# Hats in four groups of 32 rows, spreads in four row groups, one band ahead of the sampling

## What is computed

```python
x = x + _L0_conv_ref(_ln_c(x), ...)     # offsets o1, o2 and mask m by a 3x3 convolution of _ln_c(x)
...
sampled = (v00 * (1 - dy) * (1 - dx) + v01 * (1 - dy) * dx + v10 * dy * (1 - dx) + v11 * dy * dx) * mask
out = jnp.einsum('bkcp,fck->bfp', col, w).reshape(B, F, H, W)
...
t = _to_tokens(x)
t = t + _L0_ffn_ref(_ln_t(t), ...)      # softmax over 8 experts, the best two, gelu, weighted sum
```

## Time and profile before

| what | us |
|---|---|
| median of 3 runs (402.83 to 403.0) | 402.97 |
| span of the profiled execution, first to last instruction | 400.1 |
| what lies around the span, against the median | 2.9 |
| TensorE busy in the span | 315.2 |
| GpSimd busy | 228.9 |
| VectorE busy | 227.3 |
| ScalarE busy | 195.6 |

### The profile page before, as it was taken

The page is one execution under the profiler, slowest core; times in us unless marked ns, Lnnn a source line. Parts: engine busy times, 40 slices in busy tenths (PEclk is TensorE's granted clock), DMA queues, the critical chain, the costliest instruction groups (busy, mean ns, idle before and its releaser), DMA issues.

```text
span 400.1 us, 9901 instructions
## 1 busy us (share of the span) xinstructions
PE 315.2 (79%) x2395; PEld 264.9 (66%) x2395; DVE 227.3 (57%) x988; ACT 195.6 (49%) x526; POOL 228.9 (57%) x351
## 2 busy tenths in 40 slices
PE   0999799999999999999999995049989797885000
PEld 0354688888889888898898994038867686774000
DVE  3983257878778787787887876502222122332085
ACT  1253566565565665756656652314444444442063
POOL 4013043777777777777777766204777777777300
PEclk9999899999999999999999999558999999999555
DMA  8958612222222222222222220855777777762298
GB/s 209 274 164 249 265 54 75 89 80 100 78 93 85 82 99 78 90 94 76 98 84 83 95 80 26 145 139 169 223 222 243 230 231 232 227 221 72 82 315 234
DMA packets 52450, 57.88 MB, mean 145 GB/s; under 512 B 6892, under 2 KB 40423, under 8 KB 52424
## 3 DMA queue, kind: packets, MB, share of 16 engines
q1 hardware_dynamic: 45031, 48.16, 39.1%
q0 software_dynamic: 4544, 8.44, 6.6%
q10 hardware_dynamic: 2848, 0.99, 1.4%
HBM read 30.70 MB, written 14.97 MB: 114 GB/s over the span
## 4 chain that ended last, share of the span: by engine, by line
PE 53%; SPq 16%; issue 10%; DMA 6%; ACT 4%; DVE 4%; POOL 2%; ACTq 2%; DVEq 1%; POOLq 0%
PE bank L1326 18%; PE bank L1315 15%; SPq L481 5%; PE bank L1248 5%; SPq L490 4%; SPq L496 3%; DMA wide<-result 2%; PE bank L1279 2%; PE bank L1433 2%; ACT samp L758 2%; PE bank L1269 2%; PE bank L1260 2%; POOL result L658 2%; DMA routed<-padding_sb 1%; DMA result<-y,to 1%
## 5 line engine op out<-in xcount | busy, mean ns | idle before, releaser
L658 POOL DMA_INDIRECT result<-y,to x78 | 76.8, 985 | 43.8 <-DVE to L1191 26.8
L1326 PE MATMUL bank<-filt_sb,samp 128*128 128x128 f32 x576 | 79.3, 283 | 4.1 <-ACT samp L758 2.5
L1326 PEld LDWEIGHTS bank<-filt_sb,samp 128*128 128x128 f32 x576 | 69.1, 191 | 18.1 <-ACT samp L758 14.2
L1315 PE MATMUL bank<-S,xwin 100*128 100x144 f32 x512 | 78.9, 298 | 1.8 <-issue 1.7
L602 POOL DMA_INDIRECT routed<-payload,slot x64 | 63.2, 987 | 18.5 <-issue 13.5
L758 ACT ACTIVATE samp<-bank 128x432 f32<-128x432 f32 (+1 forms) x96 | 46.3, 484 | 52.8 <-PE bank L1315 52.8
L1315 PEld LDWEIGHTS bank<-S,xwin 100*128 100x128 f32 x512 | 67.7, 193 | 2.2 <-issue 2.0
L923 DVE TENSOR_TENSOR S<-ysp,bank 100x512 f32<-100x512 f32 (+1 forms) x96 | 52.5, 550 | 22.9 <-ACT ysp L729 21.8
L1433 PE MATMUL bank<-rowsT,w_blk 128*128 128x256 f32 x156 | 44.4, 408 | 13.3 <-DMA w_blk<-w_all 10.2
L1199 DVE TENSOR_TENSOR y<-bank,w_blk 128x256 f32<-128x256 f32 x39 | 16.6, 425 | 66.0 <-PE bank L1442 64.2
L822 ACT ACTIVATE rowsT<-bank 128x256 f32<-128x256 f32 x39 | 15.0, 384 | 61.0 <-PE bank L1424 61.0
(11 more groups left out here) (110 smaller groups left out, 493.1 us busy)
## 6 DMA issues: line engine op xcount, KB each, us to landing
w_blk<-w_all SPq DMA_DIRECT2D x39, 321.0 KB
xwin<-lines SPq DMA_DIRECT2D x64, 120.0 KB
xwin<-lines SPq DMA_DIRECT2D x32, 160.0 KB
rows_in<-routed SPq DMA_DIRECT2D x39, 129.0 KB
wide<-result SPq DMA_DIRECT2D x16, 256.0 KB, 4.8
w_all<-in_experts SPq DMA_DIRECT2D x4, 642.0 KB, 7.4
out_tiles<-res SPq DMA_DIRECT2D x8, 256.0 KB, 4.6
wide<-in_x_rows SPq DMA_DIRECT2D x3, 512.0 KB, 8.6
```

The lines of the kernel that those rows point to most:

```text
L658: nc.gpsimd.indirect_dma_start(result, bass.IndirectOffsetOnAxis(to[:, slot, j:j + 1].bitcast(U32), 0), y[:, slot, j, :], None, bounds_che ...
L1315: last = nc.tensor.matmul(bank[5 + (par + g) % 2][:, i * TAPS * TT:(i + 1) * TAPS * TT], xwin[:, par, t, :], weights[:, t], start=True, st ...
L1326: last = nc.tensor.matmul(bank[7][:, 0:C], samp[:, par, j, :], filt_sb[:, order[j], :], start=(j == 0), stop=(j == TAPS - 1))
```

## The change

The three parts of the hats lie in groups of 32 rows: y and x of an even tap, y and x of an odd tap, 30 rows used in each, so that the transposed hats fill 128 rows and not 120. A spread uses only the 30 rows of its group, as stationary and as moving operand. The two wide units are issued as four matmuls behind one another, and the spreads stand one band ahead of the sampling: step b spreads band b + 1. The narrow unit comes after the samples, and then the hat transposes of band b + 2. Hats, high part and split move ahead by one band too, scatter and rows of places come one band later. The place counts lie in bank 4, not in bank 7 beside the projection. VectorE's normalise writes both copies of the payload itself, into a ring of four, and GpSimd only stamps the row numbers. The diff, cut to what the loop and its start do:

```diff
-SLOT = PARTS * HATS
+GROUP = 32
+SLOT = 2 * GROUP
...
-    spread = np.zeros((2, PARTS, 2, WIN, 2, 2, Q), np.float32)
+    spread = np.zeros((2, 2, GROUP, Q), np.float32)
     q = np.arange(Q)
-    for odd in range(2):
-        for part in range(PARTS):
-            spread[odd, part, 0, q % WIN, odd, 0, q] = 1
-            spread[odd, part, 1, q // WIN, odd, 1, q] = 1
-    spread = spread.reshape(2 * SLOT, 4 * Q)
+    for part in range(PARTS):
+        spread[:, 0, part * WIN + q % WIN, q] = 1
+        spread[:, 1, part * WIN + q // WIN, q] = 1
+    spread = spread.reshape(2 * SLOT, Q)
...
-        hat3 = sb("hat3", [P, 2, TAPS + 1, SLOT], BF16)
+        hat3 = sb("hat3", [P, 2, TAPS + 1, 2, GROUP], BF16)
...
-        payload = sb("payload", [P, 2, 2, ROW])
+        payload = sb("payload", [P, QUEUED, 2, ROW])
...
-                nc.gpsimd.tensor_tensor(h3[:, 2], r, h3[:, 1], ALU.subtract).then_inc(s.hat3_ready, 1)
-
-            def pack(b, par):
-
-                pool.wait_ge(s.xn2_ready, b + 1)
-                settle(pool)
-                at_least(pool, (s.scat_even, s.scat_odd)[par], (b // 2) * 32 if isinstance(b, int) else (b - par) * 16)
-                if not isinstance(b, int):
-                    settle(pool)
-                nc.gpsimd.tensor_copy(payload[:, par, :, 0:C], xn2[:, par, :].unsqueeze(1).broadcast_to([P, 2, C])
+                nc.gpsimd.tensor_tensor(lo, r, mid, ALU.subtract).then_inc(s.hat3_ready, 1)
+
+            def stamp(b, q):
+
+                nc.gpsimd.tensor_copy(payload[:, q, :, C:C + 1].bitcast(I32), dest_sb[:, b, :].unsqueeze(2)
                                       ).then_inc(s.payload_ready, 1)
-                nc.gpsimd.tensor_copy(payload[:, par, :, C:C + 1].bitcast(I32), dest_sb[:, b, :].unsqueeze(2)
-                                      ).then_inc(s.payload_ready, 1)
-
-            def scatter(b, par):
+
+            def scatter(b, par, q):
...
+            distances(2, 0)
+            split(2, 0)
+            distances(3, 1)
...
-                distances(2, 0)
-
-                def step(b, par, _):
+                def step(b, par, _, q):
                     known = isinstance(b, int)
-                    if not known or b + 2 < BANDS:
-                        split(b + 2, par)
                     if not known or b + 3 < BANDS:
-                        distances(b + 3, 1 - par)
-                    if not known or b >= 3:
-                        scatter(b - 3, 1 - par)
+                        split(b + 3, 1 - par)
+                    if not known or b + 4 < BANDS:
+                        distances(b + 4, par)
+                    if not known or b >= 4:
+                        scatter(b - 4, par, q)
                     if not known or b >= 2:
-                        pack(b - 2, par)
+                        stamp(b - 2, (q + 2) % QUEUED)
...
+            evacuate_hatT(1)
+            hi_part(2, 0)
...
-                def step(b, par, _):
+                def step(b, par, _, q):
                     known = isinstance(b, int)
-                    if not known or b >= 1:
-                        copy_y(b, par, 0)
-                        copy_y(b, par, 1)
                     if not known or b >= 2:
                         evacuate_tokens(b - 2, par)
-                    if not known or b >= 1:
-                        copy_y(b, par, 2)
+                    if not known or b + 1 < BANDS:
+                        copy_y(b + 1, 1 - par, 0)
+                        copy_y(b + 1, 1 - par, 1)
                     evacuate_samples(b, par, 0)
-                    if not known or b + 1 < BANDS:
-                        evacuate_hatT(b + 1)
                     if not known or b >= 1:
                         std_band(b - 1, 1 - par)
                     evacuate_samples(b, par, 1)
+                    evacuate_samples(b, par, 2)
                     if not known or b + 2 < BANDS:
-                        hi_part(b + 2, par)
-                    evacuate_samples(b, par, 2)
+                        evacuate_hatT(b + 2)
+                    if not known or b + 1 < BANDS:
+                        copy_y(b + 1, 1 - par, 2)
+                    if not known or b + 3 < BANDS:
+                        hi_part(b + 3, 1 - par)
 
...
-                at_least(dve, s.t_psum, b - 1)
-                at_least(dve, s.payload_ready, 2 * (b - 1))
-                nc.vector.tensor_scalar(xn2[:, par, :], x1[:, b, :], mv1[:, par, 0:1], rs1[:, par:par + 1],
+                if not isinstance(b, int) or b >= QUEUED:
+                    dve.wait_ge((s.scat_even, s.scat_odd)[par],
+                                (b // 2 - 1) * 32 if isinstance(b, int) else (b - par) * 16 - 32)
+                nc.vector.tensor_scalar(payload[:, q, :, 0:C], x1[:, b, :].unsqueeze(1).broadcast_to([P, 2, C]),
+                                        mv1[:, par, 0:1], rs1[:, par:par + 1],
                                         ALU.subtract, ALU.mult).then_inc(s.xn2_ready, 1)
...
-                    nc.vector.tensor_tensor(place[:, :], bank[7][:, 256:256 + EXPERTS],
+                    nc.vector.tensor_tensor(place[:, :], bank[4][:, WHERE:WHERE + EXPERTS],
...
+            for link in range(3):
+                hats(2, 0, link)
...
                     other = 1 - par
-                    place_rows(b - 3, other, 0)
-                    if not known or b >= 1:
-                        multiply(b, par, 0)
-                    place_rows(b - 3, other, 1)
-                    if not known or b >= 1:
-                        multiply(b, par, 1)
-                    place_rows(b - 3, other, 2)
+                    place_rows(b - 4, par, 1)
+                    hats(b + 3, other, 0)
+                    place_rows(b - 4, par, 2)
+                    hats(b + 3, other, 1)
+                    place_rows(b - 4, par, 3)
+                    hats(b + 3, other, 2)
                     if not known or b >= 1:
                         multiply(b, par, 2)
-                    place_rows(b - 3, other, 3)
                     residual(b - 1, other, 0)
                     choose(b - 2, par, 0)
-                    hats(b + 2, par, 0)
                     residual(b - 1, other, 1)
                     choose(b - 2, par, 1)
-                    hats(b + 2, par, 1)
+                    residual(b - 1, other, 2)
                     choose(b - 2, par, 2)
-                    hats(b + 2, par, 2)
+                    place_rows(b - 3, other, 0)
+                    if not known or b + 1 < BANDS:
+                        multiply(b + 1, other, 0)
                     choose(b - 2, par, 3)
-                    residual(b - 1, other, 2)
                     choose(b - 2, par, 4)
+                    if not known or b + 1 < BANDS:
+                        multiply(b + 1, other, 1)
                     choose(b - 2, par, 5)
-                    normalise(b - 1, other)
+                    normalise(b - 1, other, (q + 3) % QUEUED)
 
...
             def transpose_hats(b, par):
                 pe.wait_ge(s.hat3_ready, b + 1)
-                if not isinstance(b, int) or b >= 3:
-                    pe.wait_ge(s.route, (b - 3) * 6 + 1)
+                if not isinstance(b, int) or b >= 4:
+                    pe.wait_ge(s.route, (b - 4) * 6 + 1)
+                if not isinstance(b, int) or b >= 5:
+                    pe.wait_ge(s.place_ready, b - 4)
                 for i in range(PAIRS):
                     last = nc.tensor.transpose(bank4b[0:2 * SLOT, i * P:(i + 1) * P],
-                                               hat3[:, par, 2 * i:2 * i + 2, :].rearrange("p k r -> p (k r)"),
+                                               hat3[:, par, 2 * i:2 * i + 2, :, :].rearrange("p k yx r -> p (k yx r)"),
                                                identb_sb[:, :])
                 last.then_inc(s.hatT_psum, 1)
 
-            def spread_hats(b, par, u):
+            def spread_taps(par, u):
+
+                slot, n, odd = (par + u) % 2, UNITS[u], u % 2
+                for yx, arrived in ((0, s.y_psum), (1, s.x_psum)):
+                    first = GROUP * (2 * odd + yx)
+                    rows = slice(first, first + PARTS * WIN)
+                    moving = hatT[rows, 4, :] if u == 2 else hatT[rows, 0:4, :].rearrange("r i t -> r (i t)")
+                    nc.tensor.matmul(bank[2 * yx + slot][0:Q, 0:n], spread_sb[rows, :], moving,
+                                     start=True, stop=True).then_inc(arrived, 1)
+
+            def spread_hats(b, par):
                 pe.wait_ge(s.hatT_ready, b + 1)
-                slot, n, odd = (par + u) % 2, UNITS[u], u % 2
-                moving = hatT[:, 4, :] if u == 2 else hatT[:, 0:4, :].rearrange("r i t -> r (i t)")
-                at_least(pe, s.y_ready, b * 3 + u - 1)
-                nc.tensor.matmul(bank[slot][0:Q, 0:n], spread_sb[:, 2 * odd, :], moving,
-                                 start=True, stop=True).then_inc(s.y_psum, 1)
-                at_least(pe, s.S_ready, b * 3 + u - 1)
```

(42 more changed lines are left out.)

113 lines of the change are left out of this document (64 added, 49 removed).

## The result

The changed kernel takes 486.58 us (median, 483.18 to 487.16) beside 402.99 for the kernel before, a ratio of 1.206 (95% interval 1.202 to 1.210). The forecast was 449.7, with a range up to 469: the direction was right, the size was not. The profiled execution has a span of 485.3 us, 85.2 above that of before.

A forecast was written before the change was run, and what follows sets the result against it. A ring of waits at 7.83 us a band, against 6.18, was taken to bound the changed kernel. 27 bands give 44.6, the ends +1.0, +1.7 and -0.6: +46.7 on 402.97 makes 449.7 us, range 440 to 469.

The forecast's parts named there:

- the ring: Loop of waits through ScalarE, GpSimd, VectorE and TensorE, once a band: 7.83 us a band against 6.18 before.
- the clock: Rival, chance 0.07: TensorE idles 2 us a band and its clock falls to half in the loop, 498 us.
- added for contention: 0.24 us a band added to the summed 7.59, for register instructions and neighbours' contention as in the old loop.
- The drain: Rival, chance 0.10: TensorE drains on entering and leaving a group of spreads, 0.64 us a band, 467 us.
- Payload: VectorE's normalise writes 256 instead of 128 elements a row: +0.13 us, beside a wait, so nothing.
- a lost cover: VectorE's normalise waits for an earlier scatter: if that landed over 2 us late, each us more would be on the ring.
- TensorE alone: TensorE's work of 5.22 us a band plus a gap of 0.3 to 0.4 would allow 5.5 to 5.6.
- the rival with the open ring: Chance 0.05: distances reach VectorE before the narrow copy is made, TensorE bounds at 5.6 us a band, 388 us.
- Ends: First sampling +1.0 us, step to the second +1.7, last three bands -0.6, chain from last sampling to plan 0.

The follow-up runs named there:

- e2_fill: The changed kernel with four matmuls that nobody reads put on TensorE between the gate and the wide spreads: 463.21 us, ratio 1.151.
- e6_scatter_early: The changed kernel with GpSimd's distances of band b + 4, scatter and stamp all moved ahead of the three subtractions: 398.66 us, ratio 0.988.

## Why the prediction was wrong: right on the ring, wrong on the clock

**The ring.** Its links, order and releasers are as forecast: a gap of 2.25 to 2.68 us behind bands at full clock, VectorE's first hat waiting 2.46 us for the distances, GpSimd waiting for the high part, the four spreads together. The two-line edit at GpSimd opens it and gives back 65 us. Its length at full clock was under-sized: 8.30 in the band shown, 8.21 in the mean of the full-clock bands and 8.18 with the filler, against 7.83. Term by term, forecast and the band from 150.17 to 158.47:

| term | forecast | measured |
|---|---|---|
| four wide spreads | 0.22 | 0.36 |
| samples | 2.10 | 2.39 |
| narrow spreads | 0.06 | 0.19 |
| transposes, until hatT starts | 0.54 | 0.49 |
| hatT evacuation, narrow copy | 0.76 | 0.75 |
| high part, three subtractions | 2.04 | 1.99 |
| distances, until the first hat | 0.54 | 0.54 |
| three hats | 0.94 | 1.20 |
| multiply and hand-over | 0.39 | 0.39 |
| added for contention | 0.24 | |
| sum | 7.83 | 8.30 |

ScalarE's and GpSimd's terms were right to 0.05. The three hats were summed as if nothing stood between them: in the rows at 156.88 to 158.08 two links of the rows of places do (L1004, L1010), 1.20 in all, and at 59.91 to 60.84, before any band has places, the same three take 0.93, the forecast. The code shows these links between the hats; the step left them out. The spreads, the samples and the narrow spreads are 0.56 longer, and 0.43 of it goes with the row groups: with full rows, in series, the samples take 2.18 and the narrow pair 0.11. The place counts, which now stand between the samples, were left out of the sum; they are 0.05.

**The drain** was a rival at 0.10 and priced at 0.64 a band. Its price is there in part: 0.14 on the four spreads (0.36 against the 0.22 of one), 0.21 on the samples (2.39 against 2.18), 0.08 on the narrow pair (0.19 against 0.11), 0.43 in all. Whether TensorE drains there, or the matmuls beside each other are slower for another reason, no run separates. The rule that was cited, the Trainium skill's TensorEngine Tiling (Array Packing), Key Properties, has the sign of these 0.43 and gives no price. The Trainium skill's 3.07 times for four row tiles (TensorE: Matmul & The Clock Gate, Part 3) is more than this case gives: 0.88 against 0.36 is 2.4 times, with the way out of the row groups in it.

**The clock** is the step that failed. It stood at 0.07, outside the sum, with the argument that each band has over 5 us of work, and that in one idle stretch of before, 244.0 to 246.4, the clock had stayed at 1.00. That row was read too early: shortly behind it the clock fell (TensorE did little in between, too),

```profile
247.60:249.80 2.20, 0.63 (x5) 0.54 (x5) 1.12 (x9) 0.04 (x1) 0.99 (x2) 0.76 0.00 0
```

and in the kernel after it is 1.00 in the gap as well and falls only in the next band. A clock of 1.00 within an idle stretch was no sign that it stays. In the loop of after the mean granted clock is 0.83, and 23.4 us go away when the gap is filled. With the ring at 8.18 and full clock the time was 463.2, inside the range; the fallen clock took it out. The rival's own price, 3.45 - 1.65 = 1.8 us, was close for a half-clock band (9.88 - 8.21 = 1.67), but it was put on every band, and only 13 of 27 were of that kind: 9.01 - 8.18 = 0.83 in the mean. In the half-clock band shown the projection at half clock, 2.45 us instead of 1.38 for ten passes, costs nothing, since TensorE still idles 0.71 behind it. A rule of the Trainium skill (TensorE: Matmul & The Clock Gate, HAM oscillation — how this bites in real kernels) describes a matmul loop whose recurring wait, longer than the gaps here, lets the clock fall in every turn; this trace agrees that a recurring wait can do it, but with gaps of 2.25 to 2.68 us and in every other turn, with 1.00 and 0.50 in two stretches of neighbouring bands.

**Payload.** "Nothing" was right for the 27 bands of the kernel after (among the last ones it cost some 2 us, below): the normalise took 0.42 instead of 0.35 (+0.07, forecast +0.13). The bound named beside it was real: once the ring was open, the scatter landed late, VectorE waited for it 21.8 us of 150, and the mean band was 6.69 instead of 5.86. The step named the price of a lost cover, and not that the cover *is* the ring: without it the wait decides.

**TensorE alone** was put at 5.22 of work and a gap of 0.3 to 0.4, 5.5 to 5.6 a band, and measured 5.85 with next to no idling. Of the 0.63 above 5.22, 0.43 go with the row groups; in place of the gap the hat transposes take 0.44 until the projection starts (154.30 to 154.74), against 0.28. So the rival with the open ring (388 us) was 10 us too hopeful: the edit that opens it gives 398.66.

**Ends.** Forecast +1.0, +1.7, -0.6 and 0; measured +4.5, +3.1, +1.1 and 0.0. The order of the start was read right, but not that the sampling of band 0 runs at half clock: its 16 passes take 4.21 us, in one row,

```profile
51.43 4.21 PE L1347 MATMUL bank<-S,xwin 100*128 100x144 f32 x16
```

where the last band of before took 2.44 for them. The first sampling itself lies between 48.5 and 51.4 in the eight kernels with the new layout; some 2 us of that are not explained by an edit, since e2_fill (49.06) starts in the same order as after (51.43). The bands at the end were put at about 5.7 each; the first took 5.80, the second 7.70 (310.85 to 318.55), since VectorE's payload there waited for a scatter, which was the condition that the forecast had named for a lost cover:

```profile
316.39 0.42 DVE L951 TENSOR_SCALAR payload<-x,mv,rs 128x256 f32<-128x256 f32 x1 [2.60 <-DMA routed<-payload,slot]
```

**The sum, put right**: 27 x (8.18 - 6.18) = 54.0 for the ring, 27 x 0.83 = 22.4 for the clock, 8.7 for the ends, 85.1 of the 85.2. Against the forecast these are 9.4 more for the ring, 22.4 for the clock that was put at nothing, and 6.6 more for the ends.

## What to carry over

When a queue is reordered, follow each wait once round through all engines: a step that waits at the head of a queue holds everything behind it, also work that has long been ready, and the cheapest cure here was the order on the engine in the middle of the ring (two lines on GpSimd, 65 us; with the scatter moved too, 88). A forecast that TensorE will idle in every turn of a loop needs a forecast of its clock beside it, and the row to look at is the work behind the idle stretch, not the stretch itself. When a ring is opened, look for the wait that it had covered: here the reuse of the payload buffers.

## What was not expected of the hardware

Gaps of 2.25 to 2.68 us at the end of turns of about 8.2 us were followed by a fall of the clock in the next band, in 13 of 14 cases; it was back at 1.00 within that band, or just behind it, so that nearly every other band ran in part at half clock. TensorE work that nobody reads made the kernel 23.4 us faster. Two matmuls in two row groups hold TensorE about as long (0.35 us) as four in four (0.36), and in the order of before, two at a time, the layout made the kernel 10.4 us slower; in the order of e6_scatter_early, four at a time and with the rest of the change, the kernel is 4.7 us faster than before.
